# Storing the result of a four-layer image kernel in three transfers

## The chip, the cores and the metric

The kernel runs on one core of a Trainium2 chip. The metric is the device time of one execution in microseconds (us). The core has five engines that take their instructions in order: PE (matrix products), DVE (vector), ACT (scalar functions), POOL, and SP, which here only issues transfers (DMAs). Engines wait for one another, and for transfers, on semaphores. A transfer adds 16 to its semaphore when it has landed.

## The reference

Sixteen images of 64 channels and 16 x 16 places pass through four residual layers: a grouped filter layer, a state-space layer, attention, and a deformable convolution. Only the last one matters here.

```python
x = x + _L0_conv_ref(_gn(x), ...)
x = x + _L1_conv_ref(_gn(x), ...)
x = x + _L2_conv_ref(_gn(x), ...)
x = x + _L3_conv_ref(_gn(x), ...)   # deformable convolution
return x                            # (16, 64, 16, 16) f32, 1 MB

# in _L3_conv_ref:
offset = conv2d(x, off_w, off_b)
mask = jax.nn.sigmoid(conv2d(x, mask_w, mask_b))
samp = deform_sample(x, offset, mask)          # bilinear, 9 taps
out = jnp.einsum('bckhw,ock->bohw', samp, weight.reshape(O, C, K * K))
return out + bias[None, :, None, None]
```

## The kernel before

The images stay on chip through all four layers in one tile, `x`, of 128 partitions (2 images of a pair x 64 channels) x 8 pairs x 256 places. In `layer3` the sampling of a tap is a matrix product with hat-shaped weights (`hats`), which POOL and ACT compute in chunks of two pairs and SP copies into place (`send_hats`, L1236).

The loop that ends the program goes over 8 pairs and 9 taps each. For a tap, PE spreads the row weights (L1500) and the column weights (L1510), ACT copies the columns (L1404), DVE multiplies (`s`, L1335) and PE multiplies by the convolution's weights and sums into `acc` (L1523). When the nine taps of pair n are summed, DVE adds them with the bias to `x[:, n]` (`add`, L1339). This add stands two taps into the next pair, and for the last pair at the very end. Nothing writes `x[:, n]` after it. The semaphore `added` starts at 2 and counts one for every add:

```python
dve.scalar_tensor_tensor(out=x[:, n, :], in0=acc[:, n % 2, 0:N], ...).then_inc(added, 1)
```

SP has nothing to issue after the `hats` of the last chunk (`next_chunk(3)`, which sends pair 6's and then pair 7's). It waits at the end of the block (L1222) for the other engines. A block of its own then stores all of `x` (L1596) and waits for the landing (L1597, in the trace L1593).

Of the kernel before, what the change touches and what calls it, by code (L numbers as in the profile page):

```python
# [24 lines left out]
NP = B // 2  # L25
# [1083 lines left out]
                        context(c, 0, k - 6)  # L1109


def layer3(nc, ins, signals, weights, x, avg2):

# [8 lines left out]
    with Memory(nc, "L3") as m:  # L1124
# [30 lines left out]
        def store_offsets(eng, quads, stored):  # L1155
            for j in range(4):
                eng.dma_start(by_place[j, 0:2 * KK, quads], off[32 * j:32 * j + 2 * KK, quads]).then_inc(stored, 16)

        def store_masks(eng, quads, stored):
            for j in range(4):  # L1160
                eng.dma_start(by_place[j, 2 * KK:, quads], sig[32 * j + 2 * KK:32 * j + 3 * KK, quads]).then_inc(stored, 16)

        def load_positions(eng, c, j):

            taps = slice(KK * j // 3, KK * (j + 1) // 3)
            for k in range(2):
                src = off_dram[ds(CH * c, CH), KK * k:KK * k + KK][:, taps].rearrange("u r n -> u (r n)").unsqueeze(0).broadcast_to([H, CH, THIRD])
                eng.dma_start(hat[C * k:C * k + C, c % 2, THIRD * j:THIRD * j + THIRD], src).then_inc(hat_in[j], 16)  # L1168

        def load_masks(eng, c, j):  # L1170
            taps = slice(KK * j // 3, KK * (j + 1) // 3)
            src = off_dram[ds(CH * c, CH), 2 * KK:][:, taps].rearrange("u r n -> u (r n)").unsqueeze(0).broadcast_to([H, CH, THIRD])
            eng.dma_start(mask[:, c % 2, THIRD * j:THIRD * j + THIRD], src).then_inc(mask_in[j], 16)

        def send_half(eng, g, e):
            src = xpad[:, 2 * g:2 * g + 2, :]
            dst = stack[:, 4 * g:4 * g + 4, :].rearrange("p (n e) s -> p n e s", e=2)
            eng.dma_start(dst[0:C, :, e, :], src[C * e:C * e + C]).then_inc(stack_in[g], 16)
            eng.dma_start(dst[C:P, :, e, 0:(HP - 1) * WP], src[C * e:C * e + C, :, WP:HP * WP]).then_inc(stack_in[g], 16)

        def send_group(eng, g):
            eng.wait_ge(xpad_ready, 2 * g + 2)
            for e in range(2):
                send_half(eng, g, e)
# [37 lines left out]
        with nc.Block() as block:  # L1222
            @block.sync
            def _(sp):
                sp.wait_ge(edge_ready, 2)
                sp.wait_ge(xpad_ready, 2)
                send_half(sp, 0, 0)
                send_group(sp, 2)

                def send_hats(b, taps=slice(0, TN)):  # L1230


                    for k in range(2):
                        for e in range(2):
                            first = C * k + 2 * b + e
                            sp.dma_start(hats[C * k:C * k + 3 * H, b, e, taps], parts[first:C * k + C:CH, :, taps]).then_inc(hats_in[b], 16)  # L1236

                def next_chunk(c):

                    sp.wait_ge(parts_ready, 3 * c + 3)  # L1240
                    for b in range(2):
                        sp.wait_ge(s_used, KK * (2 * (c - 1) + b) + 10)
                        send_hats(b)
                        if c < B // CH - 1 and b == 0:
                            for j in range(3):
                                load_positions(sp, c + 1, j)
                                load_masks(sp, c + 1, j)

                sp.wait_ge(off_ready, 1)
                store_offsets(sp, slice(0, 1), off_stored)  # L1250
                sp.wait_ge(off_ready, 2)
                store_masks(sp, slice(0, 1), off_stored)
                sp.wait_ge(off_stored, 128)
                load_positions(sp, 0, 2)
                load_masks(sp, 0, 2)
                sp.wait_ge(parts_ready, 2)
                send_hats(0, slice(0, 2 * THIRD))
                sp.wait_ge(later_stored, 128)
                sp.wait_ge(hat_in[2], 32)
                sp.wait_ge(mask_in[2], 16)  # L1260
                for j in range(3):
                    load_positions(sp, 1, j)
                    load_masks(sp, 1, j)
                sp.wait_ge(parts_ready, 3)
                sp.wait_ge(hats_in[0], 64)
                send_hats(0, slice(2 * THIRD, TN))
                send_hats(1)
                sp.wait_ge(later_stored, 256)
                for c in range(1, B // CH):
                    next_chunk(c)  # L1270

            @block.gpsimd
            def _(pool):
# [303 lines left out]
def program(nc, ins, out, layers=4):  # L1577
    Memory.semaphores = ExitStack()
    with Memory.semaphores, Memory(nc, "all") as m:
        x, avg2 = m.sb("x", [P, NP, N]), m.sb("avg2", [P, P])  # L1580
        x_out = m.sem("x_out")
        signals = NormSignals(m)
        weights = Weights(m, ins)
        with Memory(nc, "stacks") as between:
            stacks = Stacks(between)
            layer0(nc, ins, signals, weights, x, avg2, stacks)
            if layers > 1:
                layer1(nc, ins, signals, weights, x, avg2)
            if layers > 2:
                layer2(nc, ins, signals, weights, x, avg2, stacks)  # L1590
        if layers > 3:
            layer3(nc, ins, signals, weights, x, avg2)
        with nc.Block() as block:  # L1593
            @block.sync
            def _(sp):
                sp.dma_start(out.rearrange("(n e) c h w -> (e c) n (h w)", e=2), x[:]).then_inc(x_out, 16)  # L1596
                sp.wait_ge(x_out, 16)  # L1597

# [98 lines left out]
```

## Time and profile before

| | |
|---|---|
| timed runs | 527.1, 527.64 (median), 529.1 us |
| profiled execution | span 528.0 us (the profile gives no other time for it) |
| busy | PE 83%, DVE 65%, ACT 55%, POOL 25% |
| last add ends | 522.84 us |
| store issued, landed | 523.12, 527.62 us |
| bytes stored | 1,048,576, in runs of 1 KB |

All times in the trace count from the start of the span. The profiled execution's span lies 0.4 us above the median of the timed runs, and inside their spread. The chain of waits ends with the last instruction that an engine computes. The store comes after it and is seen in the views of SP and of the transfers.

### The profile page before, as it was taken

Reading aid. Unit: us, or ns where it says so; the run is one execution under the profiler, and the core shown is the slowest. Engines: PE = TensorE matmul, PEld = TensorE weight load, DVE = VectorE, ACT = ScalarE, POOL = GpSimd, SP = SyncE. Lnnn points to the kernel's source line nnn. Section 1 sums busy time; section 2 is a strip of 40 time slices with the busy share of each in tenths; the row PEclk is TensorE's granted clock in tenths of the full one; section 3 lists DMA queues with packets and bytes.
Section 4 is the critical chain, followed back from the end, with each engine's and each line's share of the span. In section 5 each row is a group of like instructions: output and inputs, shape, how many; then the busy total and the mean of one; then the engine's idle time right before and its main releaser. Section 6 shows DMA issues by size and latency. Waiting matters only on the chain. (4 is left out here: it accounts for less than half of the span.)

```text
span 528.0 us, 9368 instructions
## 1 busy us (share of the span) xinstructions
PE 439.1 (83%) x3406; PEld 231.3 (44%) x3406; DVE 342.4 (65%) x668; ACT 288.9 (55%) x511; POOL 132.8 (25%) x162
## 2 busy tenths in 40 slices
PE   0527768899999887679999999939898999999995
PEld 0216648555455664223333333324443454454442
DVE  4549876233344568978999996251654778777784
ACT  1279955131532437047878778722865578486441
POOL 4420004000000005744422212031364428065000
PEclk9956997999999988559999999957977999999999
DMA  5500000900000004952200000016390480933302
GB/s 142 164 0 1 0 0 1 197 1 1 0 1 0 1 0 107 279 175 67 73 27 3 3 2 4 0 47 160 100 226 15 89 181 2 217 55 68 67 2 79
DMA packets 20767, 33.79 MB, mean 64 GB/s; under 512 B 5657, under 2 KB 15497, under 8 KB 19957
## 3 DMA queue, kind: packets, MB, share of 16 engines
q1 hardware_dynamic: 16724, 23.70, 18.9%
q0 software_dynamic: 2176, 6.35, 4.3%
q10 hardware_dynamic: 1824, 3.19, 2.3%
q8 instruction: 26, 0.43, 0.4%
q14 instruction: 17, 0.13, 0.1%
HBM read 16.21 MB, written 4.64 MB: 39 GB/s over the span
## 5 line engine op out<-in xcount | busy, mean ns | idle before, releaser
L1335 DVE TENSOR_TENSOR L_s<-L_row_ps,L_cols 128x1024 f32<-128x1024 f32 x72 | 87.6, 1218 | 9.3 <-PE L_row_ps L1500 7.5
L910 DVE TENSOR_REDUCE L_mx<-L_ring 128x2 f32<-128x512 f32 x128 | 83.3, 686 | 12.4 <-PE L_ring L1034 11.8
L965 ACT ACTIVATE L_e<-L_ring 128x512 f32<-128x512 f32 x128 | 73.7, 597 | 21.4 <-PE L_ring L1047 19.3
L1523 PE MATMUL L_acc<-L_s,L_t_sb 128*64 128x256 f32 x576 | 81.6, 406 | 1.1 <-DVE L_s L1335 1.0
L1404 ACT ACTIVATE L_cols<-L_col_ps 128x512 f32<-128x512 f32 x72 | 42.8, 596 | 48.9 <-PE L_col_ps L1510 48.5
L1034 PE MATMUL L_ring<-stacks_k_st,stacks_q_st 64*128 64x256 bf16 x256 | 51.0, 301 | 7.0 <-DMA stacks_k_st<-L_k_parts 4.7
L1523 PEld LDWEIGHTS L_acc<-L_s,L_t_sb 128*64 128x64 f32 x576 | 36.0, 140 | 35.9 <-DVE L_s L1335 19.8
L1047 PE MATMUL L_ring<-stacks_q_st,stacks_k_st 64*128 64x256 bf16 x256 | 47.2, 282 | 1.2 <-DMA stacks_q_st<-L_m_parts 1.2
L1500 PE MATMUL L_row_ps<-L_hats,L_sel 48*128 48x512 bf16 x144 | 44.6, 392 | 0.0
L1067 PE MATMUL L_ctx_ps<-L_e,L_v_x 128*32 128x256 f32 x512 | 41.5, 398 | 0.0
L1311 DVE COPY L_t_sb<-L_acc 128x192 f32<-128x192 f32 x48 | 17.1, 357 | 31.4 <-PE L_acc L1491 31.4
L1034 PEld LDWEIGHTS L_ring<-stacks_k_st,stacks_q_st 64*128 64x128 bf16 x256 | 15.9, 98 | 43.8 <-DVE L_mx L910 24.2
L382 PE MATMUL L_y<-L_t,all_w_post 128*128 128x256 f32 x96 | 25.3, 418 | 11.5 <-DVE L_t L342 11.5
L1510 PE MATMUL L_col_ps<-L_hats,L_sel 48*128 48x512 bf16 x72 | 28.7, 400 | 7.0 <-DMA L_hats<-L_parts 5.0
L1491 PE MATMUL L_acc<-all_w_all,L_xn 64*128 64x192 f32 x96 | 26.8, 362 | 5.0 <-DVE L_t_sb L1311 2.7
L382 PEld LDWEIGHTS L_y<-L_t,all_w_post 128*128 128x128 f32 x96 | 19.4, 208 | 17.1 <-DVE L_t L342 14.2
L1491 PE MATMUL L_col_ps<-all_w_all,L_xn 64*128 64x192 f32 x96 | 26.7, 360 | 0.0
L853 POOL MEMSET L_v_x<- 128x1024 f32 x1 | 1.0, 951 | 101.7 <-POOLq L496 101.7
L1200 POOL TENSOR_TENSOR L_hat<-L_hat,L_mask 64x768 f32<-64x768 f32 x9 | 16.3, 1812 | 40.1 <-ACT L_hat L1382 40.1
L415 ACT ACTIVATE L_uu<-L_z,L_minus_mu,L_inv 128x256 f32 x48 | 24.4, 586 | 1.3 <-DVEq L314 1.3
L633 ACT ACTIVATE L_sq<-L_t_ps 128x1024 f32<-128x1024 f32 x4 | 4.1, 1024 | 34.9 <-PE L_t_ps L716 34.9
L656 PE MATMUL L_xs_ps<-L_stack,L_w_tap 128*128 128x512 f32 x48 | 22.7, 601 | 0.0
(270 smaller groups left out, 814.2 us busy)
## 6 DMA issues: line engine op xcount, KB each, us to landing
L_hats<-L_parts SPq DMA_DIRECT2D x28, 216.0 KB, 5.0
L_hat<-L_offsets SPq DMA_DIRECT2D x20, 192.0 KB, 4.7
L_mask<-L_offsets SPq DMA_DIRECT2D x10, 192.0 KB, 4.9
stacks_q_st<-L_q_parts SPq DMA_DIRECT2D x12, 128.0 KB, 3.9
stacks_k_st<-L_k_parts ACTq DMA_DIRECT2D x12, 128.0 KB, 4.8
stacks_q_st<-L_q_parts POOLq DMA_DIRECT2D x12, 128.0 KB, 2.7
stacks_k_st<-L_k_parts POOLq DMA_DIRECT2D x12, 128.0 KB, 2.9
L_stack<-L_xpad SPq DMA_DIRECT2D x7, 162.0 KB, 5.8
```

The source lines that it names most:

```text
L382: mm = pe.matmul(y2[:, ds(k, 1), :], w_post[:], t[:, q, j:j + 1, :], start=False, stop=(j == NB - 1))
L910: dve.tensor_reduce(mx[:, n % 2, :, head], ring[:, place(step) % 3].rearrange("p (q s) -> p q s", q=2), AX.X, ALU.max).then_inc(max_read, 1)
L965: act.activation(e[:, k], ring[:, 3 + v % 3], ACT.Exp, scale=HD2 ** -0.5).then_inc(e_ready, 1)
L1034: mm = pe.matmul(ring[:, place(step) % 3, q * N:(q + 1) * N], rows_of(q_st, n, h, p)[:, q * P:(q + 1) * P], rows_of(k_st, n, h, p), start= ...
L1047: mm = pe.matmul(ring[:, 3 + v % 3, t * N:(t + 1) * N], rows_of(k_st, c, h, p)[:, t * P:(t + 1) * P], rows_of(q_st, c, h, p), start=True, ...
L1067: mm = pe.matmul(ctx_ps[32 * j:32 * j + 32, g * N:(g + 1) * N], v_x[:, c % 2, t, 4 * g + j, :], e[:, 4 * g + j, t * N:(t + 1) * N], start= ...
L1335: dve.tensor_tensor(s[:, q], row_ps[:, q], cols[:, t % 3:t % 3 + 1].broadcast_to([P, 2, 2 * N]), ALU.mult).then_inc(s_ready, 1)
L1404: act.activation(cols[:, v % 3], col_ps[:, c % 2], ACT.Copy).then_inc(col_read, 1)
L1491: mm = pe.matmul(out, xn[rows, b, k // 3 * P:(k // 3 + 1) * P], w_all[rows, k % 3 * TW:(k % 3 + 1) * TW], start=True, stop=True)
L1500: mm = pe.matmul(row_ps[:, v % 2, h], sel[0:3 * H, h], hats[0:3 * H, n % 2, :, t * N:(t + 1) * N], start=True, stop=True)
L1510: pe.matmul(col_ps[:, c % 2], sel[C:C + 3 * H, 2], hats[C:C + 3 * H, n % 2, :, t * N:(t + 1) * N], start=True, stop=True).then_inc(col_rea ...
L1523: mm = pe.matmul(acc[C * e:C * e + C, b, 0:N], t_sb[:, b, h, (KK * e + t) * C:(KK * e + t + 1) * C], s[:, q, h, e * N:(e + 1) * N], start= ...
```

## The change

A helper stores a range of pairs. SP stores pairs 0 to 5 when the sixth add is done (`added` 8) and pair 6 when the seventh is done (`added` 9), both inside the sampling loop's block. The last block stores pair 7 alone, and waits until all three have landed (3 x 16 = 48).

```diff
-def layer3(nc, ins, signals, weights, x, avg2):
+def layer3(nc, ins, signals, weights, x, store_pairs, avg2):
...
                 for c in range(1, B // CH):
                     next_chunk(c)
+                for first, after in ((0, NP - 2), (NP - 2, NP - 1)):
+                    sp.wait_ge(added, 2 + after)
+                    store_pairs(sp, first, after)
...
+        def store_pairs(eng, first, after):
+            eng.dma_start(out.rearrange("(n e) c h w -> (e c) n (h w)", e=2)[:, first:after], x[:, first:after]).then_inc(x_out, 16)
...
             def _(sp):
-                sp.dma_start(out.rearrange("(n e) c h w -> (e c) n (h w)", e=2), x[:]).then_inc(x_out, 16)
-                sp.wait_ge(x_out, 16)
+                store_pairs(sp, NP - 1, NP)
+                sp.wait_ge(x_out, 48)
```

On SP, this is the end of the program, as the difference from before (128x8x256 is the whole result, 128x256 one pair):

```order
 L1236 DMA L_hats<-L_parts 48x1x2304 [waits L3_s_used]
 L1236 DMA L_hats<-L_parts 48x1x2304 x3
+L1592 DMA out_x<-all_x 128x6x256 [waits L3_added]
+L1592 DMA out_x<-all_x 128x256 [waits L3_added]
 L1222 UNCONDITIONAL_BRANCH
-L1594 UNCONDITIONAL_BRANCH [waits barrier_Pool_Activation_PE_DVE_SP_release]
-L1596 DMA out_x<-all_x 128x8x256
-L1593 UNCONDITIONAL_BRANCH [waits all_x_out]
+L1604 UNCONDITIONAL_BRANCH [waits barrier_Pool_Activation_PE_DVE_SP_release]
+L1592 DMA out_x<-all_x 128x256
+L1603 UNCONDITIONAL_BRANCH [waits all_x_out]
```

Seven of the eight pairs have moved ahead of the block's end, behind the last `hats`. No other engine's order moved. On DVE the end of the loop, where the two awaited adds (of pair 6 and, last, pair 7) stand, reads in the changed kernel:

```order
L1317 COPY L3_t_sb<-L3_acc 128x192 [waits L3_first_ready]
L1341 TENSOR_TENSOR L3_s<-L3_row_ps,L3_cols 128x1024 [waits L3_s_used,L3_col_read,L3_row_ready] x3
L1345 SCALAR_TENSOR_TENSOR all_x<-L3_acc,all_l3_vec,all_x 128x256 [waits L3_s_used]
L1341 TENSOR_TENSOR L3_s<-L3_row_ps,L3_cols 128x1024 [waits L3_s_used,L3_col_read,L3_row_ready] x7
L1345 SCALAR_TENSOR_TENSOR all_x<-L3_acc,all_l3_vec,all_x 128x256 [waits L3_s_used]
```

Between the add that releases the second store and the last add lie seven multiplications, as before (L1341 and L1345 are L1335 and L1339 of before).

## Rows read from the trace of the kernel before

**Rows 1.** Chain of waits, 519 to 528 us: start, length, what.

```profile
519.95 1.24 DVE L_s L1335
521.23 1.11 PE L_acc L1523 x8
522.36 0.48 DVE all_x L1339
```

**Rows 2.** Timeline of SP, 521 to 528 us: start, length of the issue, what.

```profile
523.12 0.43 SPq L1596 DMA_DIRECT2D out_x<-all_x  x1
```

**Rows 3.** SP's waits, 488 to 528 us: total, times, longest.

```profile
SPq L1222 <- PEq L1222: 28.9, 1, 28.9
...
SPq L1593 <- DMA out_x<-all_x: 4.1, 1, 4.1
SPq L1593 <- PEq L1593: 0.2, 1, 0.2
```

**Rows 4.** DMA issues, 515 to 528 us: count, KB, us to landing.

```profile
out_x<-all_x SPq DMA_DIRECT2D x1, 1024.0 KB, 4.5
```

**Rows 5.** Busy time by stretch of the store, with clock, DMA share, GB/s.

```profile
523.60:524.10 0.50, 0.00 (x0) 0.00 (x0) 0.00 (x0) 0.00 (x0) 0.00 (x0) 1.00 0.03 12
524.10:524.60 0.50, 0.00 (x0) 0.00 (x0) 0.00 (x0) 0.00 (x0) 0.00 (x0) 1.00 0.99 340
...
526.60:527.10 0.50, 0.00 (x0) 0.00 (x0) 0.00 (x0) 0.00 (x0) 0.00 (x0) 0.50 1.02 336
527.10:527.60 0.50, 0.00 (x0) 0.00 (x0) 0.00 (x0) 0.00 (x0) 0.00 (x0) 0.50 0.08 25
527.60:528.00 0.40, 0.00 (x0) 0.00 (x0) 0.00 (x0) 0.00 (x0) 0.00 (x0) 0.50 0.00 0
```

**Rows 6.** DMA issues, 0 to 30 us (loads at the program's start).

```profile
all_w_all<-in_w_all SPq DMA_DIRECT2D x1, 288.0 KB, 3.0
...
all_grid<-in_grid SPq DMA_DIRECT2D x1, 128.0 KB, 2.8
all_w_off<-in_w_off SPq DMA_DIRECT2D x1, 96.0 KB, 2.1
...
all_w_out<-in_w_out SPq DMA_DIRECT2D x1, 64.0 KB, 1.9
```

**Rows 7.** Timeline of SP, 364 to 370 us: small stores and what waits for them.

```profile
366.17 1.39 SPq L1161 DMA_DIRECT2D L_offsets<-L_sig  x4
368.56 1.22 SPq L1168 DMA_DIRECT2D L_hat<-L_offsets  x2
```

**Rows 8.** Line 1161 on SP: issue ns, first and last start (9 KB each).

```profile
L1161 SPq DMA_DIRECT2D L_offsets<-L_sig x4: 315/316/316, 366.2 to 367.2; - x4
```

**Rows 9.** Timeline of DVE, 493 to 511 us: the adds of pairs 5, 6.

```profile
494.24 0.47 DVE L1339 SCALAR_TENSOR_TENSOR all_x<-L_acc,all_l_vec,all_x 128x256 f32<-128x256 f32 x1
...
510.25 0.47 DVE L1339 SCALAR_TENSOR_TENSOR all_x<-L_acc,all_l_vec,all_x 128x256 f32<-128x256 f32 x1
```

**Rows 10.** Line 1236, 488 to 500 us: the hats of pair 7.

```profile
L1236 SPq DMA_DIRECT2D L_hats<-L_parts x4: 532/598/888, 491.0 to 492.8; - x4
...
DMA to landing us min/median/max: 3.5/4.3/4.9
```

**Rows 11.** Timeline of PE, 503 to 507 us: first use of those hats.

```profile
504.95 0.39 PE L1510 MATMUL L_col_ps<-L_hats,L_sel 48*128 48x512 bf16 x1
```

**Rows 12.** Busy time by stretch while those hats move (columns as Rows 5).

```profile
492.00:494.00 2.00, 2.00 (x17) 0.67 (x13) 1.63 (x2) 1.22 (x3) 0.00 (x0) 1.00 0.97 203
494.00:496.00 2.00, 2.00 (x19) 1.00 (x18) 1.87 (x3) 0.60 (x1) 0.00 (x0) 1.00 0.97 214
496.00:498.00 2.00, 2.00 (x19) 1.20 (x16) 1.48 (x2) 0.82 (x2) 0.00 (x0) 1.00 0.17 25
```

**Rows 13.** The multiplication's group, 450 to 462, then 507 to 520 us.

```profile
L1335 DVE TENSOR_TENSOR L_s<-L_row_ps,L_cols 128x1024 f32<-128x1024 f32 x7 | 8.5, 1219 | 0.5 <-PE L_row_ps L1500 0.4
...
L1335 DVE TENSOR_TENSOR L_s<-L_row_ps,L_cols 128x1024 f32<-128x1024 f32 x10 | 12.2, 1223 | 2.4 <-PE L_row_ps L1500 2.4
```

**Rows 14.** Transfers of the hats in the whole run: issue to landing.

```profile
DMA to landing us min/median/max: 2.7/4.7/8.5
```

More of the change, by code:

```diff
@@ L1591, in program @@
         if layers > 3:
-            layer3(nc, ins, signals, weights, x, avg2)
+            layer3(nc, ins, signals, weights, x, store_pairs, avg2)
         with nc.Block() as block:
```

## The prediction

> **What bounds the kernel now.** The kernel is long, but the change touches only what happens at its end, so I read the end first. The chain of waits ends with the last multiplication, its eight products and the last add, which is done at 522.36 + 0.48 = 522.84 [rows 1]. Everything behind it is one transfer. SP's timeline shows the store issued at 523.12 [rows 2], 0.28 us after the add, of which SP's waits give 0.2 to the change of blocks [rows 3]. The list of transfers says that it lands 4.5 us after its issue [rows 4], at 527.62, and the span ends 0.38 us later, at 528.0. SP's own wait agrees: 523.12 + 0.43 + 4.1 = 527.65 [rows 2, 3]. No engine computes in this time: every busy column of the stretches is zero [rows 5]. So these 5.2 us at the end are the store with its surroundings, and nothing covers them.
>
> The stretches also cut the 4.5 us into parts [rows 5]. Nearly nothing moves before 524.10 (12 GB/s in the half microsecond up to it), 336 to 352 GB/s move in the six half microseconds from 524.10 to 527.10 (the first and the last are shown), and 25 GB/s in the half behind them. The two edges carry 6 KB and 13 KB of 1,049 KB, so the steady part carries the other 1,030 KB in 3.0 us, 343 GB/s. Of the 4.5 us about 3.1 thus go with the bytes, and 1.4 do not: some 0.9 before the first byte and some 0.45 behind the last.
>
> The second thing to read is SP before the end. Its last hats go out at 492.8 [rows 10], and from then it waits 28.9 us at the end of its block, until the last add [rows 3]. It is free for both new issues.
>
> **The change, part by part.** *The last store* shrinks from eight pairs to one, 1,048,576 to 131,072 bytes. The runs stay 1 KB and the 128 partitions stay, so I let the rate and the fixed 1.4 us stand. The 917,504 bytes that are gone took 917,504 / 343e3 = 2.67 us [rows 5]. The 131,072 that stay take 0.38 us, and the store lands 1.4 + 0.4 = 1.8 us after its issue.
>
> The trace shows no lone store of 128 KB, so its landing is bounded by neighbours. Below: the four 9 KB stores of one layer's masks on the same queue. The last starts at 367.2, and SP goes on behind its wait for all at 368.56 [rows 7, 8], so a tiny store lands in at most 1.36 us, and the gain could at most be 4.5 - 1.36 = 3.1 us. That also bears out the fixed part. Above: a 128 KB load, which took 2.8 us beside other loads [rows 6], for a gain of 1.7. Farther away, the 216 KB hats of pair 7 took 4.3 us in the median and 4.9 at most, behind one another [rows 10], which would be a gain of 0.2 and a loss of 0.4. At the end nothing else moves, so I take 1.8, from the store's own rows.
>
> A page of the Trainium skill speaks against this. "DMA: Bandwidth & Descriptors" gives, in "Anatomy of one DMA — SWDGE (gpsimd) path", a fit of 2.0 us plus the bytes over 436 GB/s, most of the fixed part being the receipt of the write, and its "Rules for kernel authors" want 1 MiB or more in a transfer. For the whole store the fit makes an estimate of 4.4 us, and the trace agrees (4.5) [rows 4]; for one pair it makes 2.3 us, a gain of 2.2 and not 2.7. But the trace splits the 4.5 otherwise, since the bytes move at 343 GB/s, and about 0.45 us, not most of two, follow the last of them [rows 5].
>
> *The store of pairs 0 to 5* waits for the add of pair 5, which is done at 494.24 + 0.47 = 494.71 [rows 9]. Its 786,432 bytes take 2.3 us at the store's rate. The hats of pair 7 still move then: 214 GB/s until 496, 25 GB/s after [rows 12]. They were issued earlier on the same queue, and are needed only at 504.95 [rows 11]. They land by 492.8 + 4.9 = 497.7 at the latest [rows 10]. Should the new store hold them up by all its 2.3 us, they are there at 500.0, 4.95 us early. Cost nothing. If that cover were gone, each microsecond beyond 504.95 would be one of the program.
>
> *The store of pair 6* waits for 510.25 + 0.47 = 510.72 [rows 9] and moves 128 KB with nothing beside it. Even at the 4.5 us of the whole result it lands at 515.3, 7.8 us before the last store is issued. So at the end the count of 48 waits for the last store alone. Behind the two waits on SP nothing is queued but the end of the block, which waits for the last add anyway.
>
> *Reading x while the loop runs* could slow DVE. The multiplication took 1,219 ns in a stretch full of transfers and 1,223 in one without [rows 13], so this costs nothing. If each multiplication under the 2.6 us of early store data (two or three) were slowed by a tenth, it would cost 0.4 us.
>
> *Sum*: 528.0 - 2.67 = 525.3 for the profiled execution. The median of the timed runs lies 0.4 below its span, so I carry the difference over: 527.64 - 2.67 = 525.0.
>
> **The rivals.** *The small store keeps a longer fixed part.* The loads at the start land in 1.9 us for 64 KB, 2.1 for 96 and 3.0 for 288 [rows 6]. On the line through the last two, 128 KB take 2.1 + 32 x 0.9 / 192 = 2.25 us, for a gain of 2.25 and 525.4; by the 128 KB load itself the gain is 1.7 and the time 525.9. For it: these are landings that were measured. Against it: they run beside one another, while the store's rows show the fixed part on an idle set of DMA engines. The Trainium skill's fit, named above, would come out at the same place.
>
> *The change doesn't do what it says.* If SP passed its waits only at the end of the block, or the end waited on something other than the bytes, the time stays 527.6. Against it: SP is idle from 493 to 522, and no engine works under the store [rows 3, 5].
>
> *Slower: the early store holds up the hats of pair 7*, and PE stands at the first tap that uses them (L1510). The point is 504.95 [rows 11], 12.15 us after their last issue. The slowest hats of the whole run took 8.5 us [rows 14]; with the store's 2.3 us on top they come at 503.6, still in time. It decides only when they land more than 12.15 us after issue, and it eats the whole gain at 12.15 + 2.67 = 14.8. Three microseconds beyond that is 530.6. For it: the same 16 DMA engines carry both, which are full in that stretch (share 0.97) [rows 12]. Against it: the order of the queue, and 4.95 us of slack by the hats' own landings.
>
> **How the numbers follow.** My forecast, the bytes' time gone, has a chance of 0.70 and a range of its own of 524.3 to 525.6. The nearest to the 9 KB bound (a landing of 1.4 us, 524.5) gets 0.04, the longer fixed part (525.4 to 525.9) 0.18, no effect 0.05, and the late hats 0.03. What a measurement tells from no change is about 0.5%, 2.64 us here, so 525.0 is just that bound and the forecast falls on both sides of it: I give 0.36 of it to faster and 0.34 to the same. With the 0.04 of the lower landing, faster has 0.40. The same has 0.34 + 0.18 + 0.04 = 0.56, slower 0.03 and 0.01 of the no-effect case, as the timed runs themselves reach from 527.1 to 529.1. The range is 524.2 to 526.4: it holds both landings, the 9 KB bound within the runs' scatter, and leaves out the no-effect case and the late hats.
>
> **What would show it.** Right: the last store lands 1.8 us after its issue with some 0.4 us of data near 340 GB/s, the last add still ends near 522.8, the first store is issued at about 494.8 and the second at 510.8, PE's first use of pair 7's hats waits for no transfer, and the span is 2.7 us shorter. Wrong in size: a landing of 2.2 or more, with the extra time ahead of the first byte or behind the last one. Wrong in mechanism: a last add later than 522.9, a wait of L1510 for hats near 505, or an end that waits for one of the earlier stores.

## The result, and the profile after

The changed kernel took 524.11 us (median of 20 runs, 522.24 to 526.8) and the kernel before 527.15 (20 runs, 524.45 to 530.61) in the same comparison: a ratio of 0.9941, with a 95% interval of 0.9922 to 0.9959. The gain is 3.1 us, with 2.2 to 4.1 as bounds, so a gain of zero is ruled out. But 0.41% to 0.78% lies on both sides of the 0.5% that the prediction takes as what a measurement tells from no change, and the comparison's own verdict on the two kernels is "the same".

The profiled execution of after spans 520.8 us and that of before 528.0. That difference of 7.2 us is not the change's. To see it, cut both at three events: the load of the third chunk's first positions on SP (L1168, a quarter into the sampling loop; the expectations, which count the chunks from 0 as the kernel does, call it the second chunk's), the end of the last add, and the end of the span. These are stretches of before: start and end, length, busy time of PE, PE's weight loads, DVE, ACT and POOL with the number of instructions, PE's granted clock, DMA share, GB/s. The first two are earlier stages, cut at issues of SP (L811 to L837, and L1236 to the load named above); the last two run between the three events.

```profile
202.74:228.38 25.64, 15.69 (x70) 8.27 (x69) 22.61 (x30) 6.84 (x12) 16.73 (x19) 0.62 0.82 243
387.59:418.29 30.70, 28.73 (x188) 14.17 (x189) 18.84 (x24) 18.87 (x36) 15.22 (x9) 0.85 0.39 77
418.29:522.84 104.55, 100.57 (x759) 49.21 (x755) 80.71 (x97) 60.30 (x118) 30.43 (x18) 1.00 0.39 83
522.84:528.00 5.16, 0.00 (x0) 0.00 (x0) 0.00 (x1) 0.00 (x0) 0.00 (x0) 0.83 0.60 203
```

And the same stretches of after:

```profile
203.33:227.46 24.13, 16.18 (x75) 7.44 (x74) 22.57 (x30) 7.57 (x13) 16.78 (x19) 0.78 0.84 256
385.34:413.87 28.53, 25.12 (x177) 12.71 (x176) 17.71 (x24) 18.00 (x34) 15.18 (x9) 0.94 0.37 82
413.87:518.44 104.57, 100.67 (x759) 49.27 (x755) 80.82 (x97) 60.41 (x118) 30.43 (x18) 1.00 0.41 91
518.44:520.80 2.36, 0.00 (x0) 0.00 (x0) 0.00 (x0) 0.00 (x0) 0.00 (x0) 0.92 0.16 56
```

The early stages differ, and PE's granted clock in them too (0.62 against 0.78, 0.85 against 0.94), in code that the change doesn't touch. The loop that now has two stores in it is the same, 104.55 and 104.57 us. The tail fell from 5.16 to 2.36 us: 2.80 us. I call these two numbers the loop and the tail from here on. Taken twice of the same kernel, each repeats within 0.06 us (see the table of experiments), while the span scatters by several.

The end of after in its own rows. The chain of waits ends with the same last add as [rows 1]:

```profile
515.54 1.24 DVE L_s L1341
516.82 1.11 PE L_acc L1529 x8
517.96 0.48 DVE all_x L1345
```

SP's timeline (start, length of the issue) has the first, second and last store, and DVE's has the adds that release the first two:

```profile
490.34 0.43 SPq L1592 DMA_DIRECT2D out_x<-all_x  x1
...
506.34 0.37 SPq L1592 DMA_DIRECT2D out_x<-all_x  x1
...
518.71 0.34 SPq L1592 DMA_DIRECT2D out_x<-all_x  x1
```

```profile
489.83 0.48 DVE L1345 SCALAR_TENSOR_TENSOR all_x<-L_acc,all_l_vec,all_x 128x256 f32<-128x256 f32 x1
...
505.84 0.47 DVE L1345 SCALAR_TENSOR_TENSOR all_x<-L_acc,all_l_vec,all_x 128x256 f32<-128x256 f32 x1
```

The two stores in the loop go out 0.03 us behind their adds (489.83 + 0.48 and 505.84 + 0.47); the last one needs 0.27 us (518.44 to 518.71) because a change of blocks lies between (last_in_block, below, takes it away). The transfers, with KB and us to landing, answer to [rows 4]:

```profile
out_x<-all_x SPq DMA_DIRECT2D x1, 768.0 KB, 4.8
...
out_x<-all_x SPq DMA_DIRECT2D x2, 128.0 KB, 1.7
```

One pair lands in 1.7 us. The stretches of the tail show its parts, as [rows 5] do for the whole result: about 0.4 us between landing and the end as before (518.71 + 1.7 = 520.41, and the end at 520.8), and nearly nine tenths of the data within one half microsecond (227 GB/s x 0.5 us = 114 of 131 KB).

```profile
518.90:519.40 0.50, 0.00 (x0) 0.00 (x0) 0.00 (x0) 0.00 (x0) 0.00 (x0) 1.00 0.00 0
519.40:519.90 0.50, 0.00 (x0) 0.00 (x0) 0.00 (x0) 0.00 (x0) 0.00 (x0) 1.00 0.65 227
519.90:520.40 0.50, 0.00 (x0) 0.00 (x0) 0.00 (x0) 0.00 (x0) 0.00 (x0) 1.00 0.11 35
```

Pair 7's hats (L1236) land as in [rows 10], though the first store is issued while they still move (490.34, and the last of them lands by 488.4 + 4.9 = 493.3 at the latest), and PE first uses them 12 us after their last issue (L1516, [rows 11] before):

```profile
L1236 SPq DMA_DIRECT2D L_hats<-L_parts x4: 532/598/852, 486.6 to 488.4; - x4
...
DMA to landing us min/median/max: 3.5/4.3/4.9
```

```profile
500.54 0.39 PE L1516 MATMUL L_col_ps<-L_hats,L_sel 48*128 48x512 bf16 x1
```

It is the store that gives way: 4.8 us to landing for 768 KB, where the same transfer with nothing ahead of it took 3.7 (the run split_at_end below). DVE isn't slowed either: while the first store moves, from 490 to 494 us, its multiplication takes 1,220 ns, for the 1,219 and 1,223 of [rows 13].

```profile
L1341 DVE TENSOR_TENSOR L_s<-L_row_ps,L_cols 128x1024 f32<-128x1024 f32 x2 | 2.4, 1220 | 0.0
```

### The profile page after: what moved, and what is told of

It is laid out like the page before. It is cut to its first block and busy times, and to the rows that moved or that the text cites. A ratio compares the mean times of both kernels' runs of the same rounds, so it can differ in the third digit from the quotient of the medians.

```text
span 520.8 us, 9370 instructions
## 1 busy us (share of the span) xinstructions
PE 435.3 (84%) x3406; PEld 229.1 (44%) x3406; DVE 342.0 (66%) x668; ACT 289.0 (55%) x511; POOL 132.8 (25%) x162
## 5 line engine op out<-in xcount | busy, mean ns | idle before, releaser
L1341 DVE TENSOR_TENSOR L_s<-L_row_ps,L_cols 128x1024 f32<-128x1024 f32 x72 | 87.6, 1218 | 7.1 <-PE L_row_ps L1506 6.5
L1529 PE MATMUL L_acc<-L_s,L_t_sb 128*64 128x256 f32 x576 | 78.9, 395 | 1.4 <-DVE L_s L1341 1.2
L1516 PE MATMUL L_col_ps<-L_hats,L_sel 48*128 48x512 bf16 x72 | 27.9, 389 | 8.2 <-DMA L_hats<-L_parts 6.6
L633 ACT ACTIVATE L_sq<-L_t_ps 128x1024 f32<-128x1024 f32 x4 | 4.1, 1024 | 34.9 <-PE L_t_ps L716 34.9
```

Of the source, the lines that this page charges most:

```text
L1341: dve.tensor_tensor(s[:, q], row_ps[:, q], cols[:, t % 3:t % 3 + 1].broadcast_to([P, 2, 2 * N]), ALU.mult).then_inc(s_ready, 1)
L1516: pe.matmul(col_ps[:, c % 2], sel[C:C + 3 * H, 2], hats[C:C + 3 * H, n % 2, :, t * N:(t + 1) * N], start=True, stop=True).then_inc(col_rea ...
L1529: mm = pe.matmul(acc[C * e:C * e + C, b, 0:N], t_sb[:, b, h, (KK * e + t) * C:(KK * e + t + 1) * C], s[:, q, h, e * N:(e + 1) * N], start= ...
```

## The experiments

Theory: the bytes that left the tail are the gain, nothing else changed, and the stores in the loop are free only because of their place behind the last hats. Rivals: smaller transfers are faster in themselves; the small store keeps a longer fixed part; part of the gain lies in earlier stages.

| kernel | loop | landing of the last store | tail |
|---|---|---|---|
| before | 104.55 | 4.5 | 5.16 |
| before_again | 104.55 | 4.5 | 5.21 |
| split_at_end | 104.39 | 3.4 to 3.6 | 5.20 |
| last_four | 104.59 | 3.0 | 3.60 |
| after | 104.57 | 1.7 | 2.36 |
| after_again | 104.63 | 1.7 | 2.41 |
| last_in_block | 104.81 | 1.7 | 2.17 |
| store_before_hats | 107.86 | 1.7 | 2.39 |

(Microseconds, each from one profile. The loop starts at the load on L1168 and ends with the last add; the tail goes on to the end of the span. Four of the kernels were timed once beside a single run of before, and those times decide nothing.)

**before_again**, the kernel before, unchanged.

> The kernel before, unchanged, profiled a second time. Theory (the program up to the last add is the same in both kernels, and what differs there between the two profiles is the granted clock of that execution): the tail from the last add to the end of the span is 5.16 us again, within 0.1, and the stretch from the second chunk's loads on SP (418.29 before) to the last add is 104.55 again, within 0.1, while the span may differ from 528.0 by some us, with the difference before those loads. Rival (the change itself shortened the earlier stages, by 4.4 us): the span up to the last add is 522.8 again, within 0.5.

```profile
202.35:227.26 24.91, 15.70 (x70) 8.28 (x69) 22.63 (x30) 6.85 (x12) 16.75 (x19) 0.62 0.84 253
386.67:413.84 27.17, 27.14 (x188) 13.85 (x189) 18.82 (x24) 18.86 (x36) 15.15 (x9) 0.89 0.39 87
413.84:518.39 104.55, 100.76 (x759) 49.26 (x755) 80.75 (x97) 60.36 (x118) 30.41 (x18) 1.00 0.39 83
518.39:523.60 5.21, 0.00 (x0) 0.00 (x0) 0.00 (x1) 0.00 (x0) 0.00 (x0) 0.88 0.60 201
```

These are the stretches of before again, in a second execution. Its last add ends at 518.39, within 0.05 us of after's and 4.45 us earlier than in the first profile of the same kernel; one stage alone took 27.17 us for 30.70. What the theory says of the tail and the loop holds, and the rival falls: the 4.4 us between the last adds of the first two profiles are no more than the kernel before differs from itself. What it says of the clock isn't shown. The first stage took 25.64 and 24.91 us at the same 0.62, and the second 27.17 us at 0.89, less than after's 28.53 at 0.94. Why that stage varies so stays open.

**split_at_end**: the stores divided, but not moved.

```diff
-                for first, after in ((0, NP - 2), (NP - 2, NP - 1)):
-                    sp.wait_ge(added, 2 + after)
-                    store_pairs(sp, first, after)
...
-                store_pairs(sp, NP - 1, NP)
+                for first, after in ((0, NP - 2), (NP - 2, NP - 1), (NP - 1, NP)):
+                    store_pairs(sp, first, after)
```

> Three stores of six, one and one pairs, all issued in the last block. Theory (the gain is the bytes moved out of the tail, not the division): the bytes move one behind the other, so the tail is that of one store, 5.16 us, or up to 0.4 more for the third issue; 5.1 to 5.6. Rival (smaller transfers are faster in themselves, their fixed parts side by side): under 4.5 us. Rival (each transfer pays its fixed 1.4 us in turn): 7 to 8 us.

```profile
out_x<-all_x SPq DMA_DIRECT2D x1, 768.0 KB, 3.7
out_x<-all_x SPq DMA_DIRECT2D x2, 128.0 KB, 3.5
```

```profile
519.82 0.48 DVE L1342 SCALAR_TENSOR_TENSOR all_x<-L_acc,all_l_vec,all_x 128x256 f32<-128x256 f32 x1 [1.19 <-PE L_acc L1526]
```

The last add ends at 520.30 and the span at 525.5. The tail is 5.20 us, as with one store. A 128 KB store lands in 3.5 us when 768 KB are ahead of it, and in 1.7 alone. Both rivals fall: dividing gains nothing here, and costs nothing either. Three fixed parts of 1.4 us in turn would have made a tail of 7 to 8, so they lie over one another. The gain is the moving.

**last_four**: half of the result in the loop, half at the end.

```diff
-                for first, after in ((0, NP - 2), (NP - 2, NP - 1)):
-                    sp.wait_ge(added, 2 + after)
-                    store_pairs(sp, first, after)
+                sp.wait_ge(added, 2 + NP // 2)
+                store_pairs(sp, 0, NP // 2)
...
-                store_pairs(sp, NP - 1, NP)
-                sp.wait_ge(x_out, 48)
+                store_pairs(sp, NP // 2, NP)
+                sp.wait_ge(x_out, 32)
```

> Two stores: pairs 0 to 3 in the loop, pairs 4 to 7 (512 KB) at the end. Theory (a fixed part of about 1.3 us and the bytes at 330 to 345 GB/s): on the line between the two measured stores (1.7 us for 128 KB, 4.5 for 1,024) a landing of 2.9 us and a tail of 5.16 - 1.6 = 3.56, within 0.15. Rival (the last store of one pair gained from a fixed part that depends on the size of the issue, or from other 1 KB runs): off the line by more than 0.3 us.

```profile
out_x<-all_x SPq DMA_DIRECT2D x1, 512.0 KB, 3.0
```

```profile
517.72 0.48 DVE L1344 SCALAR_TENSOR_TENSOR all_x<-L_acc,all_l_vec,all_x 128x256 f32<-128x256 f32 x1 [1.19 <-PE L_acc L1528]
```

A landing of 3.0 us, and a tail of 3.60 (from 518.20 to the span's end at 521.8), on the line. With the 768 KB of split_at_end, which had two more stores behind it, four sizes now lie on it within 0.1 us, 128, 512, 768 and 1,024 KB at 1.7, 3.0, 3.7 and 4.5 us. From the ends the slope is 2.8 us for 917,504 bytes (328 GB/s), and 1.3 us remain for a store of nothing, by extension of the line. The landings are given to 0.1 us, so the slope is known to a few per cent (316 to 340 GB/s).

**store_before_hats**: the mechanism of the slower rival, made to happen. Four pairs are stored straight ahead of the hats of pair 6, which have no slack; the rival itself was about pair 7's, which have.

```diff
                         sp.wait_ge(s_used, KK * (2 * (c - 1) + b) + 10)
+                        if c == B // CH - 1 and b == 0:
+                            sp.wait_ge(added, 2 + NP // 2)
+                            store_pairs(sp, 0, NP // 2)
                         send_hats(b)
...
-                for first, after in ((0, NP - 2), (NP - 2, NP - 1)):
-                    sp.wait_ge(added, 2 + after)
-                    store_pairs(sp, first, after)
+                sp.wait_ge(added, 2 + NP - 1)
+                store_pairs(sp, NP // 2, NP - 1)
```

> The first store (pairs 0 to 3, 512 KB) is issued straight ahead of the hats of pair 6, on which PE already waits in the kernel before; pairs 4 to 6 follow when the seventh add is done, pair 7 at the end. Theory (the early stores cost nothing only because their place is behind the last hats, which are then 7 us early; the 16 DMA engines are shared): those hats land later by the data time of 512 KB, 524,288 / 343e3 = 1.5 us, and the issue of 0.4, PE's wait at the column product grows from 1.0 by 1.5 to 2.0 us, and the stretch from the second chunk's loads to the last add from 104.55 to 106.0 to 106.6; the tail stays 2.36. Rival (stores and hats don't hold one another up): the stretch stays within 0.5 of 104.55.

The loop is 107.86 us, 3.3 longer than after's and twice what I expected. PE's timeline of after, and then of this kernel, shows the wait for the hats, in brackets:

```profile
484.80 0.39 PE L1516 MATMUL L_col_ps<-L_hats,L_sel 48*128 48x512 bf16 x1 [1.05 <-DMA L_hats<-L_parts]
```

```profile
488.48 0.39 PE L1518 MATMUL L_col_ps<-L_hats,L_sel 48*128 48x512 bf16 x1 [2.84 <-DMA L_hats<-L_parts]
```

The wait grew by 1.8 us, inside the expected 1.5 to 2.0. The other 1.5 us come behind it. The stretches of this kernel around the wait (the number behind the five engines is the granted clock):

```profile
485.60:488.50 2.90, 0.06 (x2) 0.03 (x1) 0.01 (x1) 0.00 (x0) 0.00 (x0) 1.00 0.50 69
488.50:489.30 0.80, 0.80 (x7) 0.57 (x9) 0.12 (x1) 0.40 (x1) 0.00 (x0) 1.00 0.00 0
489.30:493.20 3.90, 3.90 (x19) 1.20 (x17) 2.59 (x3) 1.50 (x4) 0.00 (x0) 0.57 0.39 87
494.00:523.61 29.61, 28.75 (x215) 13.21 (x211) 23.40 (x26) 10.78 (x22) 0.00 (x0) 1.00 0.11 27
```

A clock of 1.00 is 2.4 GHz and 0.50 is 1.2. PE stood for 2.9 us, and from 0.8 us after it went on its clock was 0.57 in the mean for 3.9 us, mostly at the lower level, with PE busy throughout: 3.9 x 0.43 = 1.7 us of work lost. That is close to the 1.5 that the wait leaves unexplained; no run takes the clock apart from the wait. In after, PE stood 1.1 us at the same place and the clock stayed at 1.00:

```profile
483.70:484.80 1.10, 0.05 (x2) 0.01 (x1) 0.03 (x1) 0.00 (x0) 0.00 (x0) 1.00 0.08 15
484.80:490.00 5.20, 5.20 (x38) 2.20 (x38) 4.02 (x5) 2.50 (x5) 0.00 (x0) 1.00 0.41 88
```

So the place of the first store is what makes it free. Ahead of these hats even the smaller store of four pairs ate the whole gain: 3.3 lost in the loop for 2.8 in the tail.

**after_again**, the changed kernel, unchanged.

> The changed kernel, unchanged, profiled and timed again. Theory (only the tail differs): tail 2.36 us within 0.1, the stretch from the second chunk's loads to the last add 104.55 within 0.1, and the ratio to the kernel before about 1 - 2.8 / 527.15 = 0.9947, inside an interval that overlaps 0.9922 to 0.9959. Rival (part of the 3.1 us measured comes from earlier stages): a stretch shorter than 104.3, or a ratio clearly under 0.992.

```profile
520.31 0.48 DVE L1345 SCALAR_TENSOR_TENSOR all_x<-L_acc,all_l_vec,all_x 128x256 f32<-128x256 f32 x1 [1.19 <-PE L_acc L1529]
```

Loop 104.63, tail 2.41 (from 520.79 to the span's end at 523.2), and a median of 525.0 us (12 runs) against 527.08 (23 runs). The comparison gives a ratio of 0.9955, interval 0.9929 to 0.9982. The tail alone makes 1 - 2.8 / 527.1 = 0.9947, which lies inside this interval and the first one. Nothing needs a gain from earlier stages.

**last_in_block**: the last store inside the loop's block too.

```diff
-                for first, after in ((0, NP - 2), (NP - 2, NP - 1)):
+                for first, after in ((0, NP - 2), (NP - 2, NP - 1), (NP - 1, NP)):
...
-                store_pairs(sp, NP - 1, NP)
                 sp.wait_ge(x_out, 48)
```

> The third store too is issued inside the loop's block, straight behind the wait for the last add; the last block only waits for the three landings. Theory (0.24 us of the tail are the change of blocks ahead of the issue: the last store goes out 0.27 us behind the add, the second one, inside the block, 0.03): tail 2.36 - 0.24 = 2.12 us, within 0.1, loop as before, ratio to the kernel before about 0.9942, not to be told from the changed kernel's by the timed runs. Rival (the change of blocks takes as long behind the store as ahead of it, or runs under its landing either way): tail 2.36.

DVE's last add, and then SP's last store, in the timelines of this kernel:

```profile
518.55 0.48 DVE L1345 SCALAR_TENSOR_TENSOR all_x<-L_acc,all_l_vec,all_x 128x256 f32<-128x256 f32 x1 [1.19 <-PE L_acc L1529]
```

```profile
519.06 0.34 SPq L1592 DMA_DIRECT2D out_x<-all_x  x1
```

The store goes out 0.03 us behind the add, and the tail is 2.17, 0.19 to 0.24 less than in the changed kernel's two profiles: the change of blocks now runs while the bytes move. It took 523.9 us (12 runs), a ratio to the kernel before of 0.9944 with 0.9921 to 0.9967 as its interval, so a gain of zero over before is ruled out here too. A lead over the changed kernel isn't shown: its loop was 104.81, 0.2 longer than the changed kernel's, so loop and tail together are 106.98 us, and 106.93 and 107.04 in the changed kernel's two profiles. Whether the longer loop belongs to it stays open.

## Why the prediction was right or wrong

**What bounds the end: right.** The tail was the store, uncovered, and shrank with it.

**The last store: right, a little small.** I had 2.67 us gone and a landing of 1.8; it was 2.80 (2.75 to 2.85, whichever of the two profiles of each kernel is taken) and 1.7. The data time was taken from the steady middle at 343 GB/s, while the line through whole landings gives 328 and a fixed part of 1.3, not 1.4. I let the fixed part stand, but the issue itself is in it, and SP took 0.34 us to issue one pair where it took 0.43 for eight; that could be 0.09 of the 0.13 us missed, and the rest stays open. The rival of a longer fixed part, a landing of 2.25 us, fell: it was 1.7, and 1.3 for the part that doesn't go with the bytes. The Trainium skill's fit in "DMA: Bandwidth & Descriptors", "Anatomy of one DMA — SWDGE (gpsimd) path", would make an estimate of 2.3 us here, and the trace doesn't agree at this size (1.7); the fit is given for the GpSimd path, on which POOL issues the transfer, and this one is issued by SP. The neighbours that ran beside other transfers misled, the store's own stretches didn't; split_at_end shows why, as a 128 KB store behind another one takes 3.5.

**The stores in the loop cost nothing: right**, by the loop's 104.55 and 104.57. The signs that I gave as times of the trace (a last add near 522.8, stores at 494.8 and 510.8, a span 2.7 us shorter) could not be read, since all that lies ahead of the loop's start had moved by 4.4 us. From the loop's start they hold: the add of pair 5 ends 76.42 us behind it before the change (494.71 - 418.29) and 76.44 after. The reason given, the place behind the last hats, is shown by store_before_hats. My price for late hats counted the wait alone and left out the clock, which by the rows above cost nearly as much again there.

**The base of the sum: wrong.** The step that failed is "The median of the timed runs lies 0.4 below its span, so I carry the difference over: 527.64 - 2.67 = 525.0". The measured 524.11 lies 0.09 us below the lower end of my range, and the measured gain of 0.59% is on the side of 0.5% to which I gave the smaller chance, though its interval reaches over both. Of the 0.89 us between forecast and measurement 0.49 is the base: the kernel before has a median of 527.15 over 20 runs, not the 527.64 of three. 0.13 is the mis-sized term, and the other 0.27 is within the interval of the comparison. With 527.15 as the base the same sum gives 524.5. The span was no help with the base, and I read it wrongly, though the sum goes by the median of three either way. Every run that lists both has a time of 1.8 us more than its span (522.62 and 520.8 for after, 525.39 and 523.6 for before_again), so by this estimate the profiled execution of before was one of about 529.8, 2.7 above the kernel's median. A range of 0.8 us downwards left no room for three runs that scatter by 2 and for a kernel that scatters by 6. The mechanism isn't touched by this: what failed is where the sum starts.

**Faster or the same: a close call on a bound.** A gain of 2.67 us is 0.51%, and I gave 0.56 to the same, which is the comparison's verdict. With 2.80 in the tail, 0.53%, and measured ratios of 0.9941 and 0.9955, it is still close. The weight that I gave to the longer fixed part (0.18, all on the side of the same) is what tilted it, and the rows that spoke against it were in the trace of before. That rival fell, so that the likelier side came out is luck in part.

## What to carry to other kernels

A result that is stored whole at the end has its bytes' time uncovered: store each part when it is final, from a queue that is idle, behind everything that the loop still waits for, and leave only the last part and the fixed 1.3 us at the end. Dividing a transfer without moving it gained nothing. For a change of half a per cent, compare the one stretch that it touches between fixed events in both traces, and take the base from many runs.

## What the runs showed of the hardware

- Transfers on one queue cover one another's fixed part: three stores issued in a row had the tail of one (5.20 against 5.16 and 5.21 us).
- The price of a transfer that came late for PE was more than the wait: 1.8 us of extra waiting were followed by 3.9 us at a mean granted clock of 0.57, and the loop grew by 3.3.
- The same kernel, profiled twice, had its last add 4.45 us apart (522.84 and 518.39), 3.5 of it in one stage (30.70 and 27.17 us), while its last 104.55 us repeated to the hundredth.
